# Gated cross-attention and routed experts on one core: ScalarE issues the transfers of the sums, and three PSUM banks rotate

## The reference

```
qk  = einsum('bdm,bdn->bmn', qh, kh) * scale      # 8 heads x 512 x 512
sm  = softmax(qk, axis=-1)
ret = einsum('bmn,bcn->bcm', sm, vh)
x = x + tanh(g_xattn) * ret(layernorm(x), ctx, ctx)
# then, on layernorm(x), 2048 tokens, 8 experts:
logits = xt @ wg; probs = softmax(logits); idx = argmax(probs)
out = gate * (xt @ W[idx].T + b[idx])
x = x + tanh(g_ffn) * out
```

## Time and profile before

| | |
|---|---|
| median of 3 runs | 632.72 us (631.2 to 634.57) |
| profiled execution | 635.89 us |
| span of its trace | 634.3 us |
| PE, DVE | 531.7 us (84%), 422.8 us (67%) |
| ACT, POOL | 348.0 us (55%), 377.0 us (59%) |
| DMA | 90.90 MB, mean 143 GB/s |

### The profile page before, as it was taken

The page is one execution under the profiler, slowest core; times in us unless marked ns, Lnnn a source line. Parts: engine busy times, 40 slices in busy tenths (PEclk is TensorE's granted clock), DMA queues, the critical chain, the costliest instruction groups (busy, mean ns, idle before and its releaser), DMA issues. The chain is left out here.

```text
span 634.3 us, 9984 instructions
## 1 busy us (share of the span) xinstructions
PE 531.7 (84%) x2603; PEld 178.5 (28%) x2603; DVE 422.8 (67%) x831; ACT 348.0 (55%) x429; POOL 377.0 (59%) x616
## 2 busy tenths in 40 slices
PE   0489978898979889889887988989988868999994
PEld 0012212232323222232222221323222215444551
DVE  5898967677776777778786886867969464411110
ACT  3228764866858585768675757676565752111110
POOL 7465648585847566675828586868553563644541
PEclk9999989898989898999989998989979979999998
DMA  4853658474748474754716371726331152443320
GB/s 150 221 149 118 196 141 247 152 221 130 218 131 249 112 225 120 217 165 137 201 51 197 98 210 55 205 74 176 98 110 27 40 185 83 150 168 118 108 81 0
DMA packets 50391, 90.90 MB, mean 143 GB/s; under 512 B 22018, under 2 KB 24066, under 8 KB 50320
## 3 DMA queue, kind: packets, MB, share of 16 engines
q1 hardware_dynamic: 38256, 65.31, 35.9%
q0 software_dynamic: 12096, 25.13, 12.2%
HBM read 66.91 MB, written 28.41 MB: 150 GB/s over the span
## 5 line engine op out<-in xcount | busy, mean ns | idle before, releaser
L936 DVE TENSOR_REDUCE neg_max<-ps_ring 128x1 f32<-128x512 f32 x480 | 311.1, 682 | 80.7 <-PE ps_ring L1295 78.3
L847 ACT ACTIVATE probs<-ps_scores 128x1024 f32<-128x1024 f32 x256 | 250.0, 1023 | 68.8 <-PE ps_scores L1314 67.7
L1295 PE MATMUL ps_ring<-stacks 96*128 96x512 bf16 x480 | 173.9, 398 | 21.3 <-DVE neg_max L936 13.1
L1314 PE MATMUL ps_scores<-stacks 128*128 128x512 bf16 x512 | 159.1, 394 | 10.8 <-ACT probs L847 9.6
L1334 PE MATMUL ps_pv<-probs,v_ones 128*32 128x512 f32 x1024 | 144.7, 639 | 6.5 <-DVE scale L966 6.5
L1295 PEld LDWEIGHTS ps_ring<-stacks 96*128 96x128 bf16 x480 | 45.7, 99 | 179.3 <-DVE neg_max L936 126.0
L1395 PE MATMUL ps_scores<-w_sb,f_xt 128*128 x184 | 83.2, 593 | 0.0
L594 POOL TENSOR_TENSOR high_num<-high_num,scale 128x512 f32<-128x512 f32 x14 | 17.8, 1272 | 88.8 <-DMA scale<-recip_dram 88.8
L1314 PEld LDWEIGHTS ps_scores<-stacks 128*128 128x128 bf16 x512 | 47.2, 102 | 62.7 <-ACT probs L847 20.9
L624 POOL DMA_DIRECT2D stacks<-shift_parts x96 | 49.5, 519 | 20.8 <-POOL shift_parts L615 17.7
L840 ACT COPY f_xt<-ps_scores 128x512 f32<-128x512 f32 x23 | 13.5, 586 | 71.5 <-PE ps_scores L1376 71.5
(11 more groups left out here) (145 smaller groups left out, 492.2 us busy)
## 6 DMA issues: line engine op xcount, KB each, us to landing
stacks<-parts_dram SPq DMA_DIRECT2D x224, 64.0 KB, 2.3
parts_dram<-prep POOLq DMA_DIRECT2D x15, 768.0 KB
w_sb<-w_t SPq DMA_DIRECT2D x16, 512.0 KB, 6.0
recs_dram<-rec SPq DMA_DIRECT2D x16, 512.0 KB, 5.1
stacks<-parts_dram SPq DMA_DIRECT2D x32, 192.0 KB, 3.0
prep<-x_perm SPq DMA_DIRECT2D x16, 256.0 KB, 2.7
prep<-k_perm SPq DMA_DIRECT2D x16, 256.0 KB, 2.9
v_in<-v_t SPq DMA_DIRECT2D x16, 256.0 KB, 3.6
```

What stands on the lines that cost most here:

```text
L847: nc.scalar.activation(probs[:, k % 2, 2 * jp:2 * jp + 2], ps_scores[:, jp], ACT.Exp).then_inc(exp_done, 1)
L936: nc.vector.tensor_reduce(neg_max[:, g, j, c:c + 1], ps_ring[:, SLOT[tile]], AX.X, ALU.max, negate=True).then_inc(ring_free, 1)
L1295: nc.tensor.matmul(ps_ring[:, SLOT[tile]], q_stack[0:KS, into.p, g, j, c * 128:(c + 1) * 128], k_stack[0:KS, into.p, g, j], start=True, st ...
L1314: last = nc.tensor.matmul(ps_scores[:, jp, j % 2], k_stack[0:KA, B.p, g, j, c * 128:(c + 1) * 128], q_stack[0:KA, B.p, g, j], start=True, ...
```

## The change

1. `ENTRIES` is now a list without banks; entry n gets bank (1, 0, 2)[n % 3]. `turn1` stands behind `t02`, `turn0` behind `t42`, `rows` behind `t73`. TensorE issues in that order; VectorE copies the turned maxima behind (0, 2) and (4, 2), and takes the logits behind (0, 3).
2. `take_sums` moves from SyncE to ScalarE, between the two exponentials of k = 1 (sums of the batch before) and of k = 5. `invert_taken` of the second half moves from (3, 1) to (2, 2).
3. SyncE stores and spreads the inverses of the batch before first, then come weights and record. `store_recips(B, 0)` stands behind the loads of rows and keys.
4. GpSimd does `lows` right behind `rests`, and `rstd2` ahead of `load_shift` of the next batch. `norm2` moves from behind k = 6 into k = 7, `stats2` from (5, 2) to (6, 0), `norm1` from k = 1 to k = 2.
5. Batch 15 keeps the values of its second half in ring bank 1 (`last_bank`), so they don't wait for the readers of the first half; `read_low` of it moves from k = 4 to k = 5.
6. `take_ranks` frees its bank before the places are found (`find_places`), and some routing work of batches 9 to 14 moves by a few maxima.

```diff
-ENTRIES = (("t00", 1), ("turn1", 0), ("t01", 1), ("t02", 2), ("t03", 0), ("route", 1),
...
-           ("t30", 0), ("t31", 2), ("t32", 1), ("t33", 0), ("t40", 2), ("turn0", 1), ("t41", 0), ("t42", 1), ("t43", 2),
...
-           ("t70", 2), ("t71", 0), ("t72", 1), ("rows", ROWS_SLOT), ("t73", 0))
+ENTRIES = ("t00", "t01", "t02", "turn1", "t03", "route", "t10", "t11", "t12", "t13", "t20", "t21", "t22", "t23",
+           "t30", "t31", "t32", "t33", "t40", "t41", "t42", "turn0", "t43", "t50", "t51", "t52", "t53",
+           "t60", "t61", "t62", "t63", "t70", "t71", "t72", "t73", "rows")
+SLOT = {e: (1, 0, 2)[n % 3] for n, e in enumerate(ENTRIES)}
...
# SyncE, emit
+                if prev and by_transfer(B.plus(-1)):
+                    store_recips(B.plus(-1), 1)
+                    spread_recips(B.plus(-1), 1)
                 if not isinstance(B.b, int) or B.b < NB // 2:
                     load_weights(B)
                 if prev2:
                     store_record(B.plus(-2))
                 stack = not isinstance(B.b, int) or B.b + 2 < NB
-                if prev and by_transfer(B.plus(-1)):
-                    take_sums(B.plus(-1), 1)
-                    store_recips(B.plus(-1), 1)
-                    spread_recips(B.plus(-1), 1)
                 load_residual(B)
...
-                if by_transfer(B):
-                    take_sums(B, 0)
                 if stack:
                     load_stack(B.plus(2), 0)
-                if by_transfer(B):
-                    store_recips(B, 0)
                 if not isinstance(B.b, int) or B.b + 4 < NB:
                     load_rows_keys(B.plus(4))
                 if by_transfer(B):
+                    store_recips(B, 0)
                     spread_recips(B, 0)
...
# GpSimd, emit
                 if prep:
                     rests(B.plus(3))
+                    lows(B.plus(3))
...
                 split_maxima(B.plus(1), 0)
-                load_shift(B.plus(1), 0)
                 if prev:
                     rstd2(B.plus(-1))
-                if prep:
-                    lows(B.plus(3))
+                load_shift(B.plus(1), 0)
                 copy_values(B.plus(1))
...
# ScalarE
+            def take_sums(B, g):
+
+                act.wait_ge((low_read, high_read)[g], B.b + 1)
+                stand_alone(act)
+                of = (low_num[DH:128:32], high_num[0:128:32])[g]
+                act.dma_start(sums[:, g], of.rearrange("j (t c) -> j t c", c=DM // 32)).then_inc(sums_in[g], 16)
+
+            def exps(B, k, between=None):
                 for jp in range(2):
+                    if jp == 1 and between:
+                        between()
...
                 for k in range(STEPS):
-                    exps(B, k)
+                    if k == 1 and prev and by_transfer(B.plus(-1)):
+                        exps(B, k, lambda: take_sums(B.plus(-1), 1))
+                    elif k == 5 and by_transfer(B):
+                        exps(B, k, lambda: take_sums(B, 0))
+                    elif k == 7 and prev and not end:
+                        exps(B, k, lambda: norm2(B.plus(-1)))
+                    else:
+                        exps(B, k)
...
                     if k == 1 and prep:
+                        cast_high(B.plus(3), 1)
+                    if k == 2 and prep:
                         norm1(B.plus(3))
-                    if k == 2 and prep:
-                        cast_high(B.plus(3), 1)
                         cast_high(B.plus(3), 0)
...
-                    if k == 4:
+                    if k == (5 if end else 4):
                         read_low(B)
-                    if k == (5 if end else 6) and prev:
+                    if k == 5 and end:
                         norm2(B.plus(-1))
...
# TensorE, values
+                    elif B.known(NB - 1):
+                        pe.wait_ge(ring_free, ring_base(B) + 1)
                     else:
                         pe.wait_ge(low_read, B.b + 1)
                         if not by_transfer(B):
                             pe.wait_ge(low_turned, B.b - TURNED + 1)
+                into = last_bank if B.known(NB - 1) and g == 1 else ps_pv
```

More of the change, by code:

```diff
@@ L83, in holder @@
             return e, 0
-    for e in reversed(names):
+    for e in reversed(ENTRIES):
         if SLOT[e] == SLOT[name] and e != "route" and (e != "rows" or rows_in_last):
@@ L965, in turn_sums @@
                     dve.wait_ge((low_added, x1_done)[g], TURNED)
-                nc.vector.transpose(den_turned[:, g], ps_pv[:]).then_inc((low_turned, high_turned)[g], 1)
+                nc.vector.transpose(den_turned[:, g], last_bank if B.known(NB - 1) and g == 1 else ps_pv[:]).then_inc((low_turned, high_turned)[g], 1)
             def invert_sums(B, g):
@@ L1031, in take_ranks, with find_places @@
                 chain.settle()
[L1032 removed]
+                nc.vector.tensor_tensor(count[:], count[:], bank[:, n * NE:(n + 1) * NE], ALU.add).then_inc(ranks_taken, 1)
+            def find_places(group):
+                of = slice(*GROUPS[group])
+                dve.wait_ge(ranks_taken, group + 1)
+                chain.add(nc.vector.tensor_tensor(place[:, of], place[:, of], onehot[:, of], ALU.mult))
                 chain.settle()
[L1034 to L1035 removed]
                 nc.vector.reduce_sum(dest_f[:, of], place[:, of], AX.X).then_inc(placed, 1)
@@ L1340, in turn_rows @@
                 pe.wait_ge(xn2_ready, B.b + 1)
+                if isinstance(B.b, int) and B.b > RANKED[1] - 1:
+                    pe.wait_ge(logits_taken, B.b)
                 for c in range(NC):
@@ L1422, in emit @@
                         scores_for_max(B, prev, prev2, k, (0,))
-                    if k == 0:
-                        if B.known(0):
-                            pe.wait_ge(start_free, START_PAIRS)
-                        pe.wait_ge(ring_free, ring_base(B))
-                        turn_maxima(1, SLOT["turn1"])
-                    if k == NC and nxt:
-                        pe.wait_ge(ring_free, ring_base(B) + NUMBER["t40"])
-                        turn_maxima(0, SLOT["turn0"])
                     scores(B, k, 1)
@@ L1435, in emit @@
                         scores_for_max(B, prev, prev2, k, (1, 2))
+                    if k == 0:
+                        if B.known(0):
+                            pe.wait_ge(start_free, START_PAIRS)
+                        pe.wait_ge(ring_free, ring_base(B) + (NUMBER["t00"] + 1 if nxt else 0))
+                        turn_maxima(1, SLOT["turn1"])
+                    if k == NC and nxt:
+                        pe.wait_ge(ring_free, ring_base(B) + (NUMBER["t40"] + 1))
+                        turn_maxima(0, SLOT["turn0"])
                     if k > 0:
```

60 lines of the change are left out of this document (26 added, 34 removed), and 2 rows, old and new, of the table ENTRIES.

## The result

The changed kernel takes 609.85 us (median of 4 runs, 604.6 to 615.8). The kernel before, run beside it, takes 633.64 (4 runs, 631.2 to 637.3). So it is faster, as forecast. It lies inside the whole range (573 to 612) and outside the forecast's own (580 to 602): 24 us are gained where 44 were forecast. The profiled execution took 612.9 us with a span of 611.2, against 635.9 and 634.3 before: 23.1 us less span.

The account below looks back on a forecast made before the run. No engine is full; one chain from high_num through the inverses to turn_rows bounds the attention stage. Periods give -39.1 and the tail -4.7: 592.1, or 589 us at the median of runs; own range 580 to 602, whole range 573 to 612.

Parts of the forecast that it names:

- Reading by periods: Attention stage, turn1 of batch 1 to that of batch 15: 388.4 us forecast in place of 427.5.
- the 380 to 400: Sign of being right: turn1 of batches 1 and 15 lie 380 to 400 us apart.
- The sums by ScalarE: ScalarE issues the sums' transfers: start 2.7 us after high_num instead of 6.1, inverses 3 to 5 us earlier.
- rival B: Sums' transfers stay slow in flight, VectorE stands at (2,2): period 29, 611 us; chance 0.17.
- the 20 forecast: Sign of being right: add_high's wait for the inverses on GpSimd falls from 88.8 to below 20 us.
- GpSimd's circle: GpSimd's work between copies of shift, plus the shift rows' landing and a TensorE step: 25.2 to 30.5 us.
- rival A: GpSimd's circle has slack and TensorE sets the period, 25.8: 572 us; chance 0.17.
- 27.2: Forecast period of batches 1 to 12: 25.8 for the circle and half a step of waits for ScalarE.
- rival C: Slower: shift transfers behind mean2 land late, TensorE stands at each batch's first scores: 653 us; chance 0.06.
- Records and weights behind the inverses: SyncE's queue: records and weights moved behind the inverses cost zero, as nothing waits soon for either.
- VectorE under 5 us for the sums: Sign of being right: VectorE waits less than 5 us for the sums.
- The tail: Batch 15 on two banks: its second half's values no longer wait 5.54 us for VectorE's transpose; 4.7 us gained.

Follow-up runs that it names:

- lows_last: The changed kernel with GpSimd's lows and the parts' transfer at the end of its round, as before: 608.3 us, 0.963 of the kernel before.
- invert_later: The changed kernel with VectorE's inversion of the first half's sums at (7,2) instead of (6,2): 610.6 us, 0.966 of the kernel before.
- sums_by_act: The kernel before with one edit, ScalarE issuing the transfers of the sums: 620.6 us, 0.983 of the kernel before.
- the combination: The change with shift rows ahead of rstd2, weights spread over 16 rounds, low sums inverted later: 586.5 us; with weights and record ahead of the inverses, 597.5.
- weights_first: The changed kernel with weights and record ahead of the inverses on SyncE, as before: 600.9 us, 0.951 of the kernel before.
- weights_late: The changed kernel with the weights of rounds 0 to 7 loaded in rounds 8 to 15: 603.6 us, 0.945 of the kernel before.

## Why the prediction was right in kind and too high in size

**Reading by periods.** The 23.1 us of span are -23.2 between the `turn1` of batches 1 and 15, -3.5 behind them (tail) and +3.6 before them. The change moves `turn1` itself by two maxima; by the first groups of values the three parts are -21.3, -4.4 and +2.6. The distance of the two `turn1` is 404.3 us, outside the 380 to 400 that were named as the sign of being right.

**The sums by ScalarE.** Forecast: issue about 2.7 us after `high_num` is written. Measured: 230.68 against the end at 229.34, 1.3 us; it was 5.4 in the earlier trace rows. (The forecast's 6.1 counts from the start of `high_num`; so counted it is 2.0 now.) The cost of an issue, taken as 0.57, is 0.54 in this row. VectorE no longer waits for high sums. The measured 609.85 is almost rival B's price, 611, and the mean period, 404.3 / 14 = 28.9, is almost its 29. That is chance: of B's mechanism, late sums with VectorE standing at (2,2), nothing showed. The Trainium skill (DMA: Bandwidth & Descriptors, Issuing engines are not separate DMA queues) says that another issuer saves only the time that its sequencer takes to initiate the transfer. The issue itself takes 0.57 on SyncE and 0.54 on ScalarE here. What went is some 4 us in which the transfer stood behind others in SyncE's ordered queue, and that was worth 11 us over 14 batches on the kernel before. Whether the time in flight stayed, no run separates. It was 6.4 us in the earlier trace rows; in the same round of the change it is 4.9 at most (issue at 200.65, reciprocal at 205.51 without a wait), but there the weights are no longer ahead.

**GpSimd's order.** The wait for the inverses fell from 88.8 to 6.9, under the 20 forecast. The forecast gave all of that to lows and the parts' transfer, which now fill the wait; `lows_last` shows that they account for 15 of it. As forecast, GpSimd's circle through the shift rows then set the period. The term of that circle that was mis-sized is the landing, for which I took the middle between 1.5 and 2.8, 2.15, in all batches. For the last of the three transfers of a first half it is 1.6 to 1.9 in rounds 8 and 10 to 12 (2.6 in round 9), and all of these rounds but the ninth take 25.7 to 26.2, near rival A's 25.8. In the weight rounds it is 3.0 to 4.1.

At the boundary of rounds 5 and 6 the whole circle took 227.73 - 198.42 = 29.3 us, 2.1 more than 27.2. From the issue at 219.37 to the split of the next shift at 227.73 are 8.4 us, where my sum had landing and TensorE's step, 2.15 + 2.84, and 1.05 for the issue, 6.0. The stretch ahead of it, 198.42 to 219.37, took 20.95, where my sum had 19.8 and 1.4 of waits. So in this round the landing and the step behind it are all of the excess. The mean of rounds 1 to 7 is 30.5, another 1.2 longer. In batches 1 and 3 VectorE's stops for the low sums lie in that, but `invert_later` took them away and gained nothing, so this part stays open. The sum goes wrong by halves: rounds 1 to 7, forecast 7 x 27.2 = 190.4, took 213.2 (22.8 more); rounds 8 to 14, forecast 388.4 - 190.4 = 198.0, took 191.2 (6.8 less).

So the mechanism of rival C was at work in the weight rounds, with TensorE standing 2.4 to 4.0 us at the first scores of five of the seven boundaries, and rival A's period came in the plain rounds of the rest. C's own condition, a landing of 5.3 in every batch, was not reached. I had treated the spread of the earlier trace rows, 1.5 to 6.8, as one distribution with a middle, and took it to be the same in both halves of the rounds. In the new order the halves differ: the median of all transfers of line 609 is 3.3 us in rounds 1 to 7 and 1.9 in rounds 8 to 14; before, it was 3.1 and 2.7.

**Records and weights behind the inverses: cost zero.** This was wrong. "Nothing waits soon for a weight" is true, but the stacks, the parts and the shift rows share the DMA engines with it. With this order of SyncE's queue the shift rows of rounds 1 to 7 land in 3.0 to 4.1 us, with weights and record ahead of the inverses in 2.0 to 2.9, and in `sums_by_act`, with GpSimd's old order too, in 1.6. In microseconds of the whole the place of the weights is less certain (5 to 9 us in the change, the opposite in the combination).

**VectorE under 5 us for the sums.** For the high sums it waits nothing, for the low sums 14.4, which the forecast left out. `invert_later` shows that this cost nothing in the change.

**The first round.** The 3.6 us lost before batch 1 were not in the sum. With late weights the first values of batch 1 come at 73.41 instead of 76.78, so it takes the weights to lose them. It takes something of the change as well: the kernel before loads weights in round 0 too and has these values at 74.13, and `weights_first` has them at 77.21. What that is stays open.

**The tail.** Forecast -4.7, measured -4.8 in batch 15's round and -4.4 from its first values to the end of the span. Here the price was a wait seen in the trace, [5.54], and its successor was costed as well.

## What to carry to other kernels

When a wait is filled with other work, write down the circle that remains and give each transfer on it the landing of its own stage, not a median over the span. A queue's order is also the order in which loads collide: before a load is costed at nothing, ask which small transfer on the path is issued while it, or what queued up behind it, is in flight. Test one reordering at a time: here one of the change's moves (rstd2 ahead of the shift rows) gave back 14 to 16 us of what the others had gained.

## What the runs showed of the hardware

- A small transfer's landing depends on what else is in flight. The same shift rows landed in 1.6 us at a DMA share of 0.30 and in 3.3 to 4.0 at 0.95, and the slow landings moved with the weights in `weights_late`. The load that began the crowd need not be in flight any more: the weights had landed 3 us earlier.
- A stall of TensorE can cost more than its length. In the window 251.00 to 254.90 it was busy 0.02 us and its granted clock was 0.78; in the next 4 us, all busy, the clock was 0.50, the lower of the two levels (1.2 GHz). A group of eight values then takes 1.94 us, and 1.06 at full clock (312.80):

```profile
254.88 0.63 PE L1322 MATMUL ps_scores<-stacks 128*128 128x512 bf16 x1 [3.97 <-DMA stacks<-shift_parts]
...
257.79 1.94 PE L1345 MATMUL ps_pv<-probs,v_ones 128*32 128x512 f32 x8
```

In rounds 1 to 7 the clock was 0.92 on average (0.95 before), in the others 0.98 (0.96 before). After the short wait of 0.89 at 310.98 the values take 1.06, so that wait cost none of this. The earlier trace rows had shown slow values before: 1.93 behind the wait of 5.54.
